# Cross-attention on one core: score products in two 64-row strips of TensorE, keys by way of HBM, stages written out, and PSUM banks dealt out anew

## The reference, cut to what matters

```python
q = (xn @ wq.T).reshape(B, S, NUM_HEADS, HEAD_DIM)      # S = 100
k = (kvn @ wk.T).reshape(B, K, NUM_HEADS, HEAD_DIM)     # K = 1444
v = (kvn @ wv.T).reshape(B, K, NUM_HEADS, HEAD_DIM)
scores = jnp.einsum('bshd,bkhd->bhsk', q, k) * scale
attn = jax.nn.softmax(scores, axis=-1)
o = jnp.einsum('bhsk,bkhd->bshd', attn, v).reshape(B, S, D_MODEL)
return xn + o @ wo.T + bo
```

## Time and profile before

| | |
|---|---|
| median of 3 runs | 1240.93 us (1237.69 to 1241.09) |
| the profiled execution, its own time | 1242.44 us |
| its span in the trace | 1240.6 us |
| mean granted TensorE clock | 0.959 of full speed |
| TensorE matmul (PE) busy | 1059.6 us, 85% |
| TensorE weight loads (PEld) busy | 638.9 us, 51% (they overlap PE) |
| VectorE (DVE) busy | 857.3 us, 69% |
| ScalarE (ACT) busy | 825.3 us, 67% |
| GpSimd (POOL) busy | 372.6 us, 30% |

### The profile page before, as it was taken

The page is one execution under the profiler, slowest core; times in us unless marked ns, Lnnn a source line. Parts: engine busy times, 40 slices in busy tenths (PEclk is TensorE's granted clock), DMA queues, the critical chain, the costliest instruction groups (busy, mean ns, idle before and its releaser), DMA issues.

```text
span 1240.6 us, 30123 instructions
## 1 busy us (share of the span) xinstructions
PE 1059.6 (85%) x9938; PEld 638.9 (51%) x9938; DVE 857.3 (69%) x1757; ACT 825.3 (67%) x1788; POOL 372.6 (30%) x339
## 2 busy tenths in 40 slices
PE   1469888888998999988998889998999989998886
PEld 0245445445555555655555555565556556565442
DVE  5678678578766766875876657576777858777650
ACT  1237756667776777776777676657677766767565
POOL 6744433344411311330231413232242413323000
PEclk9979999899999999998999999799999999999898
DMA  7212212212221221221232120202021121201100
GB/s 187 62 37 58 61 27 58 58 30 60 65 58 33 73 74 32 72 79 38 58 77 52 39 71 21 55 24 58 22 62 35 48 61 28 61 24 31 35 3 4
DMA packets 57587, 62.92 MB, mean 51 GB/s; under 512 B 16826, under 2 KB 50906, under 8 KB 57302
## 3 DMA queue, kind: packets, MB, share of 16 engines
q1 hardware_dynamic: 57430, 60.89, 19.0%
HBM read 23.63 MB, written 0.41 MB: 19 GB/s over the span
## 4 chain that ended last, share of the span: by engine, by line
PE 58%; DVE 16%; issue 10%; ACT 10%; SPq 3%; DMA 1%; POOL 1%; DVEq 0%; ACTq 0%; POOLq 0%
PE sexp L700 15%; PE acc L719 14%; PE smax L664 12%; DVE mx L1096 7%; ACT probs L965 5%; PE shared L616 3%; PE shared L604 3%; SPq L403 2%; DVE mneg L1102 2%; PE shared L593 2%; PE shared L784 2%; PE smax L676 1%; DVE qs L1083 1%; PE shared L626 1%; SPq L469 1%
## 5 line engine op out<-in xcount | busy, mean ns | idle before, releaser
L965 ACT ACTIVATE probs<-sexp 120x400 f32<-120x400 f32 (+1 forms) x1152 | 558.9, 511 | 237.9 <-PE sexp L700 226.6
L1096 DVE TENSOR_TENSOR mx<-smax,mx 120x400 f16<-120x400 f32 (+1 forms) x1056 | 557.2, 567 | 167.7 <-PE smax L664 161.4
L700 PE MATMUL sexp<-qexp,krep 97*120 97x400 f16 (+1 forms) x1152 | 403.8, 360 | 61.1 <-ACT probs L965 41.8
L664 PE MATMUL smax<-qmax,krep 96*120 96x400 f16 (+1 forms) x1152 | 367.3, 350 | 37.5 <-DVE mx L1096 29.1
L700 PEld LDWEIGHTS sexp<-qexp,krep 97*120 97x120 f16 (+1 forms) x1152 | 152.1, 136 | 216.7 <-ACT probs L965 144.6
L719 PE MATMUL acc<-probs,vx 120*18 120x200 f32 (+1 forms) x4608 | 262.1, 347 | 1.0 <-ACT probs L965 0.9
L664 PEld LDWEIGHTS smax<-qmax,krep 96*120 96x120 f16 (+1 forms) x1152 | 157.6, 138 | 92.6 <-DVE mx L1096 51.3
L488 POOL TENSOR_TENSOR ct<-ctf,ct 128x480 f16<-128x480 f32 (+1 forms) x72 | 82.8, 1151 | 346.2 <-ACT ct L902 346.2
L719 PEld LDWEIGHTS acc<-probs,vx 120*18 120x18 f32 (+1 forms) x4608 | 109.0, 99 | 114.8 <-issue 84.5
L1094 DVE CAST mx<-smax 121x400 f16<-121x400 f32 x96 | 51.3, 570 | 120.3 <-PE smax L664 120.2
L488 POOL TENSOR_TENSOR kp<-kf,kp 128x480 f16<-128x480 f32 (+1 forms) x72 | 79.2, 1106 | 114.6 <-ACT kp L916 114.6
(11 more groups left out here) (133 smaller groups left out, 994.0 us busy)
## 6 DMA issues: line engine op xcount, KB each, us to landing
nat<-in_ctx SPq DMA_DIRECT2D x24, 720.0 KB
krep<-kp SPq DMA_DIRECT2D x576, 30.0 KB, 1.9
krep<-kp SPq DMA_DIRECT2D x288, 30.2 KB, 1.9
qexp<-qmax SPq DMA_DIRECT2D x24, 300.0 KB, 3.4
maskexp<-maskmax SPq DMA_DIRECT2D x8, 281.2 KB, 3.4
anymask<-in_mask SPq DMA_DIRECT2D x1, 1128.1 KB, 6.7
mask<-in_mask SPq DMA_DIRECT2D x8, 141.0 KB
wq<-in_w_qkv SPq DMA_DIRECT2D x1, 768.0 KB
```

Source lines behind the costliest of these rows:

```text
L664: last = pe.matmul(ps, krep[0:PARTS, u.par, t, c0:c0 + r], qmax[:, u.par, t, :, :].rearrange("p h s -> p (h s)"), start=True, stop=not masks)
L700: last = pe.matmul(ps, krep[:, u.par, t, c0:c0 + r], qexp[:, u.par, t, :, :].rearrange("p h s -> p (h s)"), start=True, stop=not masks)
L965: act.activation(probs[0:r, j % PR, :], sexp[j % SR][0:r, 0:QW], ACT.Exp).then_inc(sem["probs_ready"], 1)
L1096: op = dve.tensor_tensor(dst, src, dst, ALU.max)
```

## The change

- `PARTS` goes from 96 to 128 rows, in two strips of 64 (`STRIP`). A strip holds three blocks of 16 rows, that is two heads, in 48 rows (`KROWS`), and the row of the maximum behind them. Strip 0 has the first two heads of each group of four, strip 1 the other two.
- A score tile is now 120 keys by (two groups x two heads) x 100 queries. It takes two matmuls of 200 columns, both in the same strip; tile j is in strip j mod 2. In each step TensorE issues exponential half, maximum half, exponential half, maximum half. As `LEAD` is 13, the maximum tile is always in the other strip than the exponential tile, and it is in another bank.
- Maximum tiles run one per step: tiles 13 to 47 of `top` in steps 0 to 34, tiles 0 to 12 of `prep` in steps 35 to 47. The transposes are at steps 36 and 37, through the shared bank, the last one at 41.
- PSUM: `SR` goes from 2 to 3 banks `sexp`; `smax` keeps 3, `acc` 1; all other products have the one bank `shared`. `BANK` and `BANK3` are gone.
- `qmax` and `qexp` become one tile `qx` for both passes, in three copies by unit; the copying DMA is gone, the maximum goes into two rows with two DMAs. `mx` has two copies.
- Keys go from `kp` to HBM (`kept`, 3 DMAs per unit) and from there to `krep` (18 DMAs per unit). ScalarE waits for the write to `kept` alone.
- The loops and the registers are gone: every stage is written out. The `If` on TensorE is still there, one stage earlier (`MASK_STAGES`).

The core of the diff:

```diff
-PR, SR, MR = 10, 2, 3
-PARTS = 3 * 32
+PR, SR, MR = 10, 3, 3
+PARTS = 128
+STRIP = 64
+KROWS = 48
-VALUES_AT = [j // TOGETHER * TOGETHER + TOGETHER + 1 for j in range(NSTEP)]
-MAX_AT = [i * 39 // NSTEP for i in range(NSTEP)]
-MT_AT = 39
+VALUES_AT = [j // TOGETHER * TOGETHER + TOGETHER + SR - 1 for j in range(NSTEP)]
+LEAD = 13
-        shared = [psum(f"shared{i}") for i in range(2)]
+        shared = psum("shared")
+        def tile_of(j):
+            return j // T, j // 2 % 2, j % 2
+        def max_tile(s, j):
+            u, i = (s.top, j + LEAD) if j + LEAD < NSTEP else (s.prep, j + LEAD - NSTEP)
+            return (u, i) if u is not None else None
-                for t in range(T):
+                for i in range(2):
                     for j, part in enumerate((0, 0, 1)):
-                        sp.dma_start(krep[32 * j:32 * j + 32, u.par, t, c0:c0 + n],
-                                     kp[32 * t:32 * t + 32, part, c0:c0 + n]).then_inc(sem[f"krep_in{g}"], 16)
+                        at_row = STRIP * i + 16 * j
+                        sp.dma_start(krep[at_row:at_row + 16, u.par, :, c0:c0 + n],
+                                     kept[u.par, :, part, c0:c0 + n].rearrange("(t i r) n -> i r t n", t=T, i=2)[i]
+                                     ).then_inc(sem[f"krep_in{g}"], 16)
-                last = pe.matmul(ps, krep[:, u.par, t, c0:c0 + r],
-                                 qexp[:, u.par, t, :, :].rearrange("p h s -> p (h s)"), start=True, stop=not masks)
+                last = pe.matmul(ps[:, 2 * S * a:2 * S * a + 2 * S],
+                                 krep[at_row:at_row + KROWS + 1, u.par, 2 * tp + a, c0:c0 + r],
+                                 qx[at_row:at_row + KROWS + 1, u.third, 2 * tp + a, :, :].rearrange("p f s -> p (f s)"),
+                                 start=(a == 0 or not masks), stop=not masks, skip_group_check=masks)
...
             def stage(s, n, masks=False):
                 for j in range(NSTEP):
-                    if s.exp is not None:
-                        exp_scores(s.exp, j, masks and s.exp.L == 1)
-                    for i in range(NSTEP):
-                        if MAX_AT[i] == j and s.top is not None:
-                            max_scores(s.top, i, masks and s.top.L == 1)
+                    m = max_tile(s, j)
+                    for a in range(2):
+                        if s.exp is not None:
+                            exp_product(s.exp, j, a, masks and s.exp.L == 1)
+                        if m is not None:
+                            max_product(*m, a, masks and m[0].L == 1)
```

More of the change, by code:

```diff
@@ L244, in build, with at @@
             READ[f"mk{g}"] = ("mask_ready", g + 1)
[L246 to L267, removed]
+        def at(name, u, k):
+            return sem[name], max(B * sum(PER[name][:u.L]) + PER[name][u.L] * u.batch + k, 0)
         def groups():
@@ L300, in pipeline @@
             while n <= last:
[L301 to L304, removed]
-                    with engine.Fori(1, 4, 2) as b:
-                        enter_loop(n, units, b)
-                        run(stage_of(n, units, b, n), n)
-                        run(stage_of(n + 1, units, b, n), n)
-                        leave_loop(n, units, b)
-                    n += 4
-                else:
-                    run(stage_of(n, units), n)
-                    n += 1
-        def bank(use, u):
-            return BANK3[use] if u is not None and u.L >= 2 else BANK[use]
-        held = [None, None]
-        def last_uses(s):
-            ends = [(AT["v1"], "v1", s.top), (AT["mk2"], "mk2", s.prep if s.prep.L == 1 else None),
-                    (AT["mn"], "mn", s.top), (AT2["o"], "o2", s.att2)]
-            for _, use, u in sorted((x for x in ends if x[2] is not None), key=lambda x: x[0]):
-                held[bank(use, u)] = (use, u)
+                run(stage_of(n, units), n)
+                n += 1
+        held = [None]
         def await_read(pe, i):
@@ L450, in stage @@
                 if s.prep is not None:
+                    for g in range(3):
+                        keep_keys(s.prep, g)
                     replicate(s.prep, 0, s.exp, NSTEP // 3)
@@ L636, in queries @@
             def queries(u):
[L638 removed]
+                pe.wait_ge(*at("x_lo", u, 1))
                 ps = begin("q", u)
@@ L869, in stage @@
                         queries(s.prep)
-                    if s.top is not None and j == MT_AT:
-                        maxima(s.top)
+                    for i in range(2):
+                        if s.top is not None and j == AT[f"mt{i}"]:
+                            maxima(s.top, i)
                     if s.top is not None and j == AT["mn"]:
@@ L1207, in stage @@
                 for j in range(NSTEP):
-                    for i in range(NSTEP):
-                        if MAX_AT[i] == j and s.top is not None:
-                            maximum(s.top, i)
+                    m = max_tile(s, j)
+                    if m is not None:
+                        maximum(*m)
                     if s.post is not None and j == AT["O"] + 1:
@@ L1226, in stage @@
                             power(s.load, part)
-                    if s.top is not None and j == MT_AT:
-                        for i in range(2):
+                    for i in range(2):
+                        if s.top is not None and j == AT[f"mt{i}"]:
                             maxima(s.top, i)
```

484 lines of the change are left out of this document (237 added, 247 removed).

## The result

| | before | after |
|---|---|---|
| median of the runs beside each other (4 and 4) | 1241.01 us | 1539.6 us (1526.57 to 1564.34) |
| ratio after / before, 95% interval | | 1.2375 [1.2261, 1.2489] |
| span of the profiled execution | 1240.6 us | 1562.6 us |
| mean granted TensorE clock in it | 0.959 | 0.727 |
| TensorE's waits in it, all together | 170.1 us | 298.5 us |

The profiled execution of after is the slowest of its four and counts as a slow run, so the ratio is of the other three, which had clocks of 0.749, 0.763 and 0.766 at 1547.5, 1531.7 and 1526.57 us. The forecast was 1268 us, with a range of 1170 to 1350: slower was the forecast's likelier side (0.62), but by 2%, not by 24%.

What follows compares the result with a forecast made beforehand. TensorE was taken to bound every stage. From 1242.4 us: -161 score products, +80 changes of form, +182 one bank, -58 coming back, -18 loops, -8 keys, +9 clock, +26 in sum, gave 1268 us, range 1170 to 1350.

Steps and rivals of the forecast that it cites:

- score products: TensorE's score products in strips: a step falls from 0.346 to 0.20 us, 161 us gained over 48 steps x 23 stages.
- changes of strip form: TensorE switching between strip products and products in the shared bank: 883 new changes at 0.09 us, 80 us lost.
- one bank, less what comes back: TensorE waits for readers of the single shared bank, 182 us lost, less 58 us of other waits that fill up.
- loops: Three loops written out: no back jumps of 3.1 us nor half clock behind them, 18 us gained.
- keys by HBM: Fewer key copies at the start, so the first exponential product comes earlier, near 82 us: 8 us gained.
- clock: TensorE's granted clock with TensorE at about 78% busy: 1% off 900 us, 9 us lost.
- under 30 ns apart in pairs: Sign in TensorE's timeline: how close neighbouring strip products start; the alternatives were 50 to 60 ns, or 85 (no overlap).
- strips do not overlap: Rival: products on different rows do not run at once, the 161 us gain goes, 1429 us; chance 0.11.
- The first rival: Strips nearly free: step 0.172 us, changes of form cost nothing, 1188 us; chance 0.27 together with small bank waits.
- The one bank costs less than counted: Rival: shared-bank waits cost 130 us instead of 182, 1216 us; chance 0.27 together with strips nearly free.
- the clock falls: Rival: stages with 16 us of TensorE waits let the clock fall to a mean of 0.88, 1340 us; chance 0.12.
- stages of layer 0 grow by 7: Sign against the forecast: layer 0 stages longer by 7 us would mean that strip products do not overlap.

## Why the forecast missed

The sum again, each term with what the traces gave in its place. Waits are TensorE's totals. For the clock: at a mean granted clock c the half rate took 2 x (1 - c) of the span, 102 us before and 853 after, 751 more; TensorE works 80% of it and would have needed half of that, 751 x 0.80 / 2 = 300 us.

| term | forecast | found | how |
|---|---|---|---|
| score products | -161 | -194 | 0.346 to 0.17 us, x 48 x 23 |
| changes of strip form | +80 | +83 | 922 changes into and out of strips from full-height products, x 0.09 |
| one bank, less what comes back | +124 | +128, loop jumps in it | waits 170.1 to 298.5 us |
| loops | -18 | -18 | alone, 1222.6 for 1241 |
| keys by HBM | -8 | +3 | first exponential product at 93.36, was 90.54 |
| clock | +9 | +300 | above |
| sum | +26 | about +317 | measured: span +322 |

The sum of what was found counts the loops once, in the waits and the clock, and leaves out the keys' 3 us, whose wait is in the 128. It leaves out one thing more: the second pair that starts 0.045 us late behind a change. With 527 changes from full height into strips that is about 24 us at full clock, an estimate; so the sum closes to some 20 us and no better. The 300 is of the profiled execution; the same working with the mean clock and span of the other three (0.759, 1533.5 us) gives about 255.

**Score products.** The overlap was right, and a step among strips came out at the upper end of the gain. Of the signs named, starts "under 30 ns apart in pairs" came true. That a weight load costs 0.056 us where pairs run side by side was wrong: among strips it costs nothing that shows. Behind a change of form the second pair comes 0.045 us late, for a reason that was not tested.

The rival "strips do not overlap" fell; the nearest thing to it, all four halves in one strip with the one bank, is 1782.8 us and not 1429, again for the clock. The Trainium skill (TensorE: Matmul & The Clock Gate, LDWEIGHTS) gives 100 ns for a load of 120 columns; the rows contradict that as a rate, with two loads in each 0.085 us, or in 0.13 behind a change.

**Changes of form.** 922 against 883, and 0.09 us each: right, but for the late second pair. The first rival (1188 us) had the step right at 0.17 us and the changes wrong, which it took as free.

**One bank.** Right in place and within a tenth in size: the waits ahead of shared products for ScalarE or VectorE grew by 200 us (37.5 to 237.3), for 182 forecast and 214 counted. Stage 16 was to wait 17 us and has 17.7 ahead of shared products, stage 9 5.7 and has 7.6. What comes back is there too, if smaller: waits for `probs` fell from 41.8 to 15.7 us and those of the maximum products for `mx` from 29.1 to 10.7, together 44 of 58. That the net came out at 128 for 124 is in part luck, for the 128 also has in it 10 us of waits at the loops, which the forecast counted in another term. "The one bank costs less than counted" fell.

**Loops.** Right. No straight stretch of after waits for instructions except at the `If`, once, 3.4 us.

**Keys by HBM.** The sign was wrong, and 11 us lie between forecast and found. SyncE's queue is free at 49.7 us, where it was at 57.8. But before the change ScalarE had waited only this long for the copies (ScalarE's timeline of the kernel before):

```profile
59.15 0.56 ACT L916 COPY kf<-shared 128x484 f32<-128x484 f32 x1 [2.84 <-DMA krep<-kp]
```

2.84 us were to be had, not 8. The one bank took them back, in the filling (TensorE's timeline of after):

```profile
36.97 1.36 PE L549 MATMUL shared<-ct,wk 128*128 128x480 f16 x3 [1.20 <-ACT kp L871]
39.53 0.40 PE L579 MATMUL shared<-ident,xcur 100*128 100x100 f32 x1 [1.20 <-ACT kp L871]
40.65 1.16 PE L587 MATMUL shared<-xT,wq 128*128 128x100 f16 x12 [0.72 <-DVE xT L1028]
```

The query products start at 40.65 and not, as before, at 37.10. The step that failed is that SyncE's queue was taken for what ends the filling, from its length in the earlier trace rows, where the wait behind it had to be read. With two shared banks the first exponential product starts at 89.68 us, and with 64 rows at 88.98, 1.5 us earlier than before: the one bank took 3.7 us there, and the keys' way through HBM costs nothing, as said.

**Clock.** This is the step that failed, and by the table it is nearly the whole miss (291 of 296 us): "At about 78% I take 1% off 900 us: 9 us." It went by one relation, busy share to granted clock, read from two stretches in which all products had 96 rows or more. No row of the trace of before showed a stretch full of products of few rows, and the text did not say so. For the strips' time it had given both ends since no row showed them; for their clock it had none. The rival "the clock falls" had the right consequence with the wrong mechanism and half the reach: it took 0.88 from waits alone, and waits alone give 0.91. With the one bank and strips of 64 rows it is 0.86, and with 48 and 49 rows 0.73 (0.75 to 0.77 in the other executions): this last and largest part, 110 us, is the height of the products. What takes 0.91 to 0.86 stays open. With 0.91 on the change, 2 x 0.09 x 1320 = 238 us would be at half rate, 136 more than before, at 0.80 / 2 a price of 54 us: 1242 - 194 + 83 + 128 + 54 = about 1313 us, inside the range. This is worked out and was not run.

"The forecast is wrong if stages of layer 0 grow by 7, which would mean no overlap": the first six stages grew by 5 on the mean (44.7 to 50.0 us), stages 4 and 5 by 9.7 and 12.6, and stage 9 by 7.7, with full overlap, so that sign would have misled. With two banks stage 9 takes 40.9 us at a clock of 1.00, 2.5 less than before: the strips do what they were to do wherever the clock holds.

**What stays open.** Why strips of 64 rows side by side have a lower clock than full height, and whether the changes of form have a part in it. Why the clock falls deeper in the stages with layer 2, and in the last three, also at 64 rows (0.86 in the former). Whether it is the rows that a product names or the work in them: the 16 rows added were zero on one side only, and another filling wasn't tried.

## What to carry to other kernels

Before a product is cut to fewer rows to run beside another, price TensorE's clock as its own unknown: a stage in which TensorE is 96% busy can still run at half clock for much of its time. If rows are free, let the product use all 64 of its strip, with zeros on one side; that gave 57, 110 and 151 us here, in the three pairs of runs. A single PSUM bank for all small products is paid for with the rest of the reader's time at each use, and that sum can be worked out from the trace beforehand.

## What the runs showed of the hardware

- Two products in different 64-row strips, in different banks, start 3 ns apart in the median. Pairs that follow one another are 0.08 to 0.09 us apart for 200 columns at full clock, with their weight loads hidden; the second pair behind a product of another form starts 0.13 us after the first.
- A change between full-height, row-strip and column-strip products costs 0.09 us each way at full clock.
- The granted clock was lower with fewer rows at an equal or higher busy share: over the twelve stages without layer 2, 0.99 at 96 and 97 rows (91% busy), 0.88 at 64 (92%), 0.70 at 48 and 49 (94%), all without strips side by side within a step. Between the last two only the height differs.
- Rows that hold only zeros on the query side (the moving operand) still raised the clock: 0.82 to 0.892 with two banks side by side.
- Cutting 400 columns into two products of 200 at full height cost 6 us at most, within the runs' spread: 1228.5 us and a clock of 0.974 against 1222.6 and 0.973.
